# One table for all side stages of a fused attention and FP4 feed-forward kernel

## The reference

```
k_eff = (W_dq.T @ W_uq.T @ W_uk).reshape(nh, hs, n_kvl)
c_kv = x @ W_dkv.T
q = (x @ W_dq.T @ W_uq.T).reshape(B, T, nh, hs)
q_lat = einsum('bqhd,hdl->bhql', q, k_eff)
attn = softmax(where(causal, einsum('bhql,bkl->bhqk', q_lat, c_kv) / sqrt(hs), -inf))
y = einsum('bhql,hld->bqhd', einsum('bhqk,bkl->bhql', attn, c_kv), v_eff)
x = layernorm(x + y)
# feed-forward; qd(v): blocks of 16: scale = max(max|v| / 6, 1e-12), v / scale to the
# nearest of 0, .5, 1, 1.5, 2, 3, 4, 6 with its sign, times scale
h = silu(qd(x) @ qd(w_gate).T) * (qd(x) @ qd(w_up).T)        # 352 wide
x = layernorm(x + qd(h) @ qd(w_down).T)
```

## Time and profile before

| | us |
|---|---|
| median of 3 runs | 753.1 (752.66 to 756.08) |
| the profiled execution | 758.44 |
| its span in the trace | 756.6 |
| TensorE busy | 563.6 (74%) |
| VectorE busy | 532.3 (70%) |
| ScalarE busy | 412.3 (54%) |
| GpSimd busy | 316.0 (42%) |
| mean granted clock of TensorE | 0.876 |

### The profile page before, as it was taken

The page is one execution under the profiler, slowest core; times in us unless marked ns, Lnnn a source line. Parts: engine busy times, 40 slices in busy tenths (PEclk is TensorE's granted clock), DMA queues, the critical chain, the costliest instruction groups (busy, mean ns, idle before and its releaser), DMA issues.

```text
span 756.6 us, 15168 instructions
## 1 busy us (share of the span) xinstructions
PE 563.6 (74%) x5863; PEld 254.3 (34%) x5863; DVE 532.3 (70%) x981; ACT 412.3 (54%) x598; POOL 316.0 (42%) x441
## 2 busy tenths in 40 slices
PE   4275988589787888788888889696978897862623
PEld 2132333233333434333333334242323342421412
DVE  0389787388889767788788778888787784264461
ACT  2311766377665766565576666564656675742220
POOL 4520032000436654433337464533273536258682
PEclk9655999799998999999898999998899998995565
DMA  3393006602300192020300480203000000000000
GB/s 101 77 241 101 2 3 151 145 2 51 94 5 12 31 210 56 15 52 16 92 16 2 90 196 11 56 10 78 3 16 3 3 2 16 1 15 0 0 14 15
DMA packets 34222, 37.91 MB, mean 50 GB/s; under 512 B 6390, under 2 KB 19766, under 8 KB 34150
## 3 DMA queue, kind: packets, MB, share of 16 engines
q1 hardware_dynamic: 33238, 36.39, 20.0%
q10 hardware_dynamic: 912, 0.54, 0.3%
HBM read 19.64 MB, written 16.78 MB: 48 GB/s over the span
## 4 chain that ended last, share of the span: by engine, by line
PE 39%; DVE 31%; POOL 13%; issue 10%; ACT 4%; DMA 2%; SPq 1%; POOLq 0%; DVEq 0%; ACTq 0%
DVE top L837 19%; PE yt_ps L556 11%; PE ring L537 6%; PE ring L520 5%; PE misc L495 3%; PE ring L507 2%; PE misc L466 2%; POOL eg L1151 2%; POOL hx L1123 2%; POOL hx L1121 2%; POOL hx L1125 1%; DVE z L906 1%; PE misc L455 1%; PE misc L486 1%; DVE hc L963 1%
## 5 line engine op out<-in xcount | busy, mean ns | idle before, releaser
L837 DVE TENSOR_REDUCE top<-ring 128x2 f32<-128x1024 f32 (+3 forms) x384 | 349.6, 948 | 113.4 <-PE ring L507 80.2
L715 ACT ACTIVATE probs<-ring 128x1024 f32<-128x1024 f32 x288 | 293.8, 1027 | 132.1 <-PE ring L507 79.7
L556 PE MATMUL yt_ps<-probs,v_op 128*32 128x512 f32 (+3 forms) x1536 | 171.6, 520 | 0.5 <-ACT probs L715 0.5
L537 PE MATMUL ring<-q_op,k_op 59*128 59x512 bf16 (+3 forms) x768 | 124.0, 346 | 50.2 <-DVE top L837 40.3
L520 PE MATMUL ring<-k_op,q_op 56*128 56x512 f16 (+3 forms) x768 | 127.8, 355 | 44.5 <-ACT probs L715 18.9
L520 PEld LDWEIGHTS ring<-k_op,q_op 56*128 56x128 bf16 x768 | 38.4, 96 | 171.0 <-issue 116.8
L1144 POOL TENSOR_TENSOR r<-r,yq 128x128 f32<-128x128 f32 x32 | 14.6, 457 | 168.3 <-DVE yq L876 168.3
L537 PEld LDWEIGHTS ring<-q_op,k_op 59*128 59x128 f16 x768 | 37.7, 95 | 120.8 <-DVE top L837 58.7
L507 PE MATMUL ring<-ident,mask_s 64*128 64x64 bf16 x1024 | 59.5, 198 | 0.0
L507 PEld LDWEIGHTS ring<-ident,mask_s 64*128 64x128 bf16 x1024 | 47.7, 102 | 17.7 <-issue 5.0
L507 PEld LDWEIGHTS ring<-ident,mask_t 64*128 64x128 bf16 x1024 | 47.2, 100 | 18.2 <-issue 6.8
(11 more groups left out here) (170 smaller groups left out, 758.4 us busy)
## 6 DMA issues: line engine op xcount, KB each, us to landing
q_op<-scratch_q SPq DMA_DIRECT2D x32, 224.0 KB
k_op<-scratch_k SPq DMA_DIRECT2D x32, 224.0 KB
scratch_k<-k_part SPq DMA_DIRECT2D x32, 192.0 KB, 3.3
scratch_q<-q_part SPq DMA_DIRECT2D x32, 128.0 KB, 3.1
scratch_q<-q_part SPq DMA_DIRECT2D x16, 192.0 KB, 3.3
xp<-in_L_attn_x_dram SPq DMA_DIRECT2D x4, 512.0 KB, 4.4
r<-in_L_attn_x_dram SPq DMA_DIRECT2D x8, 256.0 KB, 2.8
out_dram<-z SPq DMA_DIRECT2D x8, 256.0 KB, 2.3
```

The source lines that it names most:

```text
L537: last = nc.tensor.matmul(ring[slot][:, e, at:at + n], k_op[lo:lo + rows, pair, j * P:(j + 1) * P], q_op[lo:lo + rows, pair, (c + 1) * CHU ...
L556: last = nc.tensor.matmul(yt_ps[32 * q:32 * (q + 1), lo:CHUNK], v_op[:, j, 4 * a + q, :], probs[:, (STEPS * a + tile) % P_RING, q % 2, at: ...
L715: nc.scalar.activation(probs[:, n % P_RING, :, :], ring[(2 * n + 1) % 3][:, :, :], ACT.Exp, scale=SCALE).then_inc(t_exp.sem, 1)
L837: last = nc.vector.tensor_reduce(top[:, kc, :, p, i], ring[slot][:, :, at:at + n], AX.X, ALU.max)
```

## The change

The lists and offsets become one table, `events`, read by every engine through `events_at`. The stages are divided into smaller pieces: statistics in two halves and a mean, inverse, mask and rounding each at a step of its own, logarithm and exponential of the sigmoid apart. The gates are no longer evenly spaced (4, 10, 18, 24, 30, 36, 44, 49; before 4, 10, 16, 22, 28, 34, 40, 46), the transposes of h follow 11 to 13 steps after their gate (before 16), and jobs of the next batch are moved: k to 11 and 12 (12, 15), q to 22 and 26 (18, 24), v to 14 and 16 (19, 25).

Both norms leave VectorE: GpSimd does them in two operations over 512 columns with broadcast mean and inverse root. So do the scale and the magic factor. The mask becomes a tensor_tensor with a broadcast constant, the widened scale a scalar_tensor_tensor. The ring of probabilities has eight tiles, six of the twelve weighing steps are one earlier, and SP's store of the first output half stands behind the maxima of quad 3 and the operand reads after them. A wait of ScalarE for the rows of maxima counts all six of a quad.

```diff
-P_RING = 6
+P_RING = 8
...
-    W_STEP = [3, 5, 6, 7, 9, 10, 12, 14, 16, 17, 18, 19]
+    W_STEP = [3, 5, 5, 6, 8, 10, 12, 14, 16, 17, 17, 18]
...
+    GATE = (4, 10, 18, 24, 30, 36, 44, 49)
+    UP = (7, 13, 19, 25, 33, 37, 47, 51)
+    HT = (15, 23, 29, 35, 41, 48, 55, 60)
...
+    for t, (g, u, ht) in enumerate(zip(GATE, UP, HT)):
+        events += [(g, "gate", -1, t), (u, "up", -1, t), (g + 1, "clamp", -1, t), (g + 2, "ln", -1, t), (g + 3, "sig", -1, t),
+                   (g + 4, "h", -1, t), (g + 5, "amax", -1, t), (g + 6, "hinv", -1, t), (g + 7, "hdiv", -1, t),
+                   (g + 8, "hexp", -1, t), (g + 9, "hround", -1, t), (ht, "ht", -1, t)]
...
-                if b > 0:
-                    sp.wait_ge(fin_v.sem, fin_v.at(b - 1, 0))
-                    sp.dma_start(out[b - 1, 0:CHUNK].rearrange("(n p) c -> p n c", p=P), z[:, 0, :, :]).then_inc(stored[0].sem, 16)
                 max_rows_in(b, 3)
                 if b + 1 < B:
                     operands_in(b + 1, 2)
+                if b > 0:
+                    sp.wait_ge(fin_p.sem, fin_p.at(b - 1, 0))
+                    sp.dma_start(out[b - 1, 0:CHUNK].rearrange("(n p) c -> p n c", p=P), z[:, 0, :, :]).then_inc(stored[0].sem, 16)
+                if b + 1 < B:
                     residual_in(b + 1, 0)
...
+            def h_exponent(b, t):
+                n, g = t % 2, b * NT + t
+                dve.wait_ge(hd_p.sem, hd_p.at(b, t))
+                if g >= 2:
+                    dve.wait_ge(hr_p.sem, g - 1)
+                nc.vector.tensor_tensor(hc[:, n, :, :].rearrange("p n k -> p (n k)").bitcast(U32), hx[:, n, :, :].rearrange("p n k -> p (n k)").bitcast(U32),
+                                        exponent[:, :].to_broadcast([P, FF]), ALU.bitwise_and).then_inc(he_v.sem, 1)
...
+            def rounded(dst, magic, sc_, ready, s0, s1, s2, s3, b, k):
 
                 pool.wait_ge(ready.sem, ready.at(b, k))
+                nc.gpsimd.tensor_scalar(magic, magic, 1.0, ROUND, ALU.max, ALU.mult).then_inc(s0.sem, 1)
+                pool.wait_ge(s0.sem, s0.at(b, k))
                 nc.gpsimd.tensor_tensor(dst, dst, magic, ALU.add).then_inc(s1.sem, 1)
...
+            def normalised(dst, src, mean, scale, sub, done, b, k):
+
+                sh = [P, PER, C]
+                nc.gpsimd.tensor_tensor(dst, src, mean.unsqueeze(2).to_broadcast(sh), ALU.subtract).then_inc(sub.sem, 1)
+                pool.wait_ge(sub.sem, sub.at(b, k))
+                nc.gpsimd.tensor_tensor(dst, dst, scale.unsqueeze(2).to_broadcast(sh), ALU.mult).then_inc(done.sem, 1)
```

More of the change, by code:

```diff
@@ L148, in build, with events_at @@
+    def events_at(b, n):
+        return [(kind, b + d, k) for s, kind, d, k in (events if b < B else tail) if s == n and 0 <= b + d < B]
     with ExitStack() as ctx:
@@ L1171, in _ @@
                         values(b + 1, VALUES_AT.index(n))
-                    for kind, jb, k in jobs_at(b, n):
-                        if kind == "q":
-                            parts(jb, 2 + k)
-                        if kind == "yn":
-                            residual(jb, k)
-                    if n in K_REST_AT and b + 1 < B:
-                        parts(b + 1, K_REST_AT.index(n))
                     if b < B:
```

398 lines of the change are left out of this document (211 added, 187 removed).

## The result

The changed kernel takes 832.6 us (median of 4 runs, 830.7 to 839.1), the kernel before 754.0 beside it: a ratio of 1.106, with a 95% interval of 1.099 to 1.112. Medians and ratios here leave out the executions that lay more than 1.5% above the fastest of the same kernel, which matters for one run alone, e13. The forecast had the sign right and the size wrong: 765, with 777 as the upper end of its range.

What follows compares the result with a forecast made beforehand. TensorE was nearest its limit in the body, GpSimd in the tail's loop. Body -21, SP +10, weighing +3, tail +18 and clock +2 gave +12 on 753.1: 765 us, ratio 1.016, range 744 to 777.

Steps and rivals of the forecast that it cites:

- the -21: Step loop of the body: named waits worth 30 us removed, against 9 us of new waits on GpSimd, net -21.
- the wait at step 18: Body, TensorE's wait before the q projection with its slow clock: 2.8 + 3 us in two batches, 12 us gained.
- the clamp waits: Body, waits for GpSimd's clamp: 2.4 us each, four counted, 10 us gained.
- The factor: Magic factor on GpSimd: 1.53 us for each of eight tail tiles, 12.2 us, all on the tail's chain.
- 9 for everything new on GpSimd: Body, new waits on GpSimd: 2 us per batch at steps 11 to 20 and 1 for x's rounding.
- Rival C: GpSimd sets the body's pace, each of 24 tiles making TensorE wait 0.7 us; 773 us, chance 0.16.
- C's sign: Middle batches: the logarithm and the gate product wait on GpSimd in every tile.
- SP: SP's row of issues holds step 36's exponential 27.9 us behind step 26's in three batches; +10 us.
- Weighing and `yn`: Weighing one step earlier nearly ties with the copy of `yt` in 16 quads: 0 to +8, booked +3; `yn` unpriced.
- The mask: Two-input mask on VectorE: 0 to 0.1 us of loss for each of 32, on an idling engine, booked as nothing.
- The tail: After the last exponential, GpSimd is in the loop; new factor, scale and norms there add 18 us.
- Clock: Lower clock behind a longer wait at step 36 in two batches, +2 us.

Runs made afterwards that it cites:

- e13: Kernel before with the exponent masks of x and the hidden tiles written as two-input operations; 761.9 us, ratio 1.008.
- e12: Kernel before with SP issuing the maxima rows of quad 2 between the scratch writes of quads 0-1 and those of quads 2-3; 746.2 us, ratio 0.986.
- e19: e10 with the exponent masks back in the one-input form; 729.7 us, ratio 0.966.
- e10: e9 with SP's queue reordered as in e12; 734.2 us, ratio 0.972.
- e9: e4 with `yn` and the weighing steps back at the places of the kernel before, the ring left at eight; 763.5 us, ratio 1.011.
- e4: Changed kernel with only the magic factor back on VectorE; 777.4 us, ratio 1.035.
- e17: e14 with the exponent masks back in the one-input form; 736.4 us, ratio 0.977.
- e14: e10 with the slices of both norms back on VectorE and two steps of the second half's statistics moved; 746.7 us, ratio 0.988.
- e15: Changed kernel with only SP's queue reordered as in e12; 810.4 us, ratio 1.074.
- e16: Kernel before with only the new weighing steps and the ring of eight, `yn` left at its old steps; 764.7 us, ratio 1.013.
- e2: Kernel before, with its old lists and masks, and only the norms, scales and magic factor moved to GpSimd; 788.1 us, ratio 1.050.
- e1: Changed kernel with norms, scales and magic factor back on VectorE, the second half's statistics a step earlier; 781.0 us, ratio 1.040.

## Why the prediction was wrong, point by point

*The body.* The loss from the kernel before to the changed one is taken apart by a chain of runs. Dividing SP's queue gives 8 to 10 us (e12), and the rest of the change in e19 another 16.5 (729.7 against 746.2). Then come 4.5 us for the masks (e19 to e10), 29.3 for the row on SP left whole (to e9), 13.9 for `yn` and the weighing (to e4) and 55.2 for the factor (to the changed kernel). Another order of the same edits could share them out otherwise. The gain of 16.5 includes a tail that is 5.7 us longer (96.4 against 90.7), so e19's body gains some 22, about the -21 that I had written. How it divides is only partly shown: 7 to 12 us are the norms (e17 to e19, e10 to e14), and no run sets the wait at step 18 or the clamp waits apart. What sank the forecast is that costs were booked at a fraction, the factor's above all.

*The factor* is the largest of them. I had booked its 12 us in the tail and, in the body, 2 us per batch at step 11 to 20 and 1 for x, 9 for everything new on GpSimd. It cost 14.5 in the tail and 41 in the body. The price of one operation was about right (1.53 estimated, 1.40 measured), and so was GpSimd's busy time (427, forecast 425 to 430). The step of the prediction that failed is this term of 9 us for new waits on GpSimd in the body. At steps 13 to 20 of the third batch the queue runs without a pause for 22.9 us (417.73 to 440.64), and I had even counted 19 of them out from rows; I weighed them against the steps up to the logarithm, and not against what waits behind the waiting engine: mask, then gate product, then `misc`, then TensorE, and the transposes of the rounded tiles (38.4 us). Rival C came nearest, with 0.7 us a tile; divided by 24 tiles, the factor alone cost 1.7 in the body. But C's sign, that the logarithm waits on GpSimd in every tile, did not come: it waits in 8 of 24, less than before. C's price, and mine, also left out that with the waits the clock falls: e4 has 0.94 and 0.96 in its third and fourth stretch, the changed kernel 0.88 and 0.90. The Trainium skill (GPSIMD Engine Reference, section "Performance versus the Vector engine") gives a two-input add of 2048 columns as 1.96 times slower on GpSimd than on VectorE; the rows bear it out for two-input work of 352 columns (0.93 us for the product on GpSimd, 0.51 for the two-input mask on VectorE). For this factor, with one input and two operations, the difference is larger still: 1401 ns on GpSimd, 346 as VectorE's median in the kernel before.

*SP.* This term was right, mechanism and size: I forecast 27.9 us from the exponential of step 26 to that of 36, and the changed kernel takes 28.0, 28.7 and 28.1 in its first three batches; the waits at step 36 are 12.0 in the first and 4 to 5 in the next two, as forecast. The three make 84.8 us, 11 more than the 73.8 of the earlier trace rows, where I had booked 10. What the sum did not say is what the whole row is worth: 22 us in e15 and 29 in e10, of which the kernel before had 8 to 10 already. It took the kernel before as the base, in which the same steps were slow for other reasons. Once these go (e10 needs 20 us from step 26 to 36), the row on SP is the limit for all that they would have won. A bound of this kind is worth the distance to the next limit and not to today's time.

*Weighing and `yn`.* I booked 3 of 0 to 8 us for the copy of `yt`. On the kernel before it is 9.8 us of waits and 10 of time (e16), outside my range; in the changed kernel the wait is 2.6 us, near the 3. `yn`, one step earlier, I had not priced at all, though it reads a copy that ScalarE makes in the step before: 21.5 us of waits and 30 of time on the kernel before, 16.3 us of waits in the changed one. There the two together are worth 14 to 18 us (e4 to e9), by the waits mostly `yn`, the term that was put at nothing.

*The mask.* "Nothing" was some 5 to 10 us. The step took the nearest mean, 492 ns, from the earlier trace rows as the duration of the old form. That mean mixes 0.33 us with 1.05 for the masks that wait for GpSimd; the new form is 0.51 and 1.23. The 878 ns that I set beside it are such a mean too: the median of that row is 748. The lock of the Trainium skill that I cited (SBUF — State Buffer, "SBUF: two separate sides") is what the two pairs of tail rows show: either form waits until GpSimd's product has ended. The Trainium skill (VectorE: DVE Perf Modes, section "The TRN2 errata") gives (N+151)/0.96 ns for a float32 add with two inputs. For 352 columns that is an estimate of 524 ns by that page, and the trace's 0.51 to 0.53 agrees.

*The tail.* Forecast 107 to 111, measured 113.6; a period of 8.2 us, measured 8.05. The clamps of two tiles in a row:

```profile
756.50 1.09 POOL L1182 TENSOR_SCALAR eg<-eg 128x352 f32<-128x352 f32 x1 [0.57 <-ACT eg L698]
...
764.55 1.09 POOL L1182 TENSOR_SCALAR eg<-eg 128x352 f32<-128x352 f32 x1 [0.57 <-ACT eg L698]
```

The chain in the earlier trace rows was the right one. Between these tiles only the factor lengthens it, by 1.42 us: in e4, with the factor on VectorE and the scale still on GpSimd, the clamps come at 709.54 and 716.16, a period of 6.62 as in the kernel before. So the scale (0.32) is hidden in the idle time ahead of the clamp, which is 1.15 us in the earlier trace rows and 0.58 in e4. The engine part of the sum was nearly right too: e2, with the old lists and masks, has a tail of 111.1, 19.8 more than before, where 20.2 were added up and 18 booked. The rest comes with the table and the masks, for which nothing was booked: e1 has 93.4 against 91.3, and the mask's form alone makes 1 to 2 us (e13 92.3 against 91.3, e10 98.5 against e19's 96.4).

*VectorE* is busy 492 us in place of 470 to 480: the first norm's slices were cheaper (374 ns) than those of the second from which I took them, and the masks dearer.

*Clock.* +2 was the smallest term and among the most wrong. The windows put the longer busy time of the same matmuls at 8.8 and 5.2 us in the second and third stretch; it is part of the costs above, not beside them.

The gap before the q projection at step 18 is gone, as forecast. At the batch's end a wait of 2.0 us at step 70 is left in the third batch. The error is first of all the factor in the body, 41 us where everything new on GpSimd had 9, then the worth of the row on SP to the rest, and `yn` and the masks, put at nothing. All lie where an engine that works in order waits for another.

## What to carry to other kernels

A cost on an engine with idle time is priced by the queue at the step where it lands, and by whatever stands behind the engine that waits for it; follow that row until it reaches the bound engine. A job that reads another engine's result needs a step between them even when the trace shows a tie: moved one step closer on the kernel before, it was lost in every quad. And take a duration from instances in the same surroundings, not from a group's mean.

## What the runs showed of the hardware

A float32 tensor_scalar with two operations of 352 columns takes 1.40 us on GpSimd and 1.92 with 512 columns, more than a two-input operation of the same size (0.93 and 1.27); the clamp with one operation takes 1.10. The scale of 22 columns takes 0.32.

VectorE and GpSimd hold each other up in both directions, and it shows as duration and not as idle time. These are single instances beside the usual durations, without a run that sets the cause apart. In the timeline above, the clamp at 434.56 began while VectorE's two-input mask ran (434.51 to 435.03) and took 1.43 us in place of 1.10, and the subtraction at 426.56 took 1.61 in place of 1.27. Beside that subtraction VectorE's widened scale, 22 columns in the two-input form that the change gave it, took 1.26 us, where the median of its 32 instances is 0.17:

```profile
426.95 1.26 DVE L947 SCALAR_TENSOR_TENSOR h_wide<-h_amax,least 128x22 f32<-128x22 f32 x1
```

What stays open: why the table and the engine changes cost more together (79) than the sum of the two (66), which no run takes apart; and whether the ring of eight does anything, since it was never changed alone.
